# A two-layer graph network: its two node stages, run over chunks of seven blocks before, run block by block after, with their constants folded into the weights

## The chip, the cores and the metric

One core of a Trainium2 chip. The metric is the device time of one launch in microseconds (us).

## The reference, cut to what matters

There are 6250 nodes with 128 channels and 100,000 edges, each with 16 attributes. Linear layers are written as functions here.

```
msg  = relu(relu(m1(x)[src] + m2(x)[dst] + me(edge_attr)) @ W_net.T + b_net)   # 96 channels an edge
agg  = segment_max(msg, src)                   # 96 channels a node, 0 where none
x    = layernorm(x + x @ W_o1.T + b_o1 + agg @ W_o2.T + b_o2)      # first node stage
h    = gelu(concat(x[src], x[dst]) @ eW1 + eb1);  message = h @ eW2 + eb2
aggregated = segment_sum(message, dst)
upd  = gelu(concat(x, aggregated) @ nW1 + nb1) @ nW2 + nb2
x    = layernorm(x + (x + upd))                                     # last node stage
```

`layernorm` takes mean and variance over the 128 channels of a node, adds 1e-5 to the variance and divides by its root.

## The kernel before, in words

All numbers are float32 where nothing else is said. Nodes lie in NB = 49 blocks of 128; the edges pass in G = 208 groups of four steps of 128. The kernel is a row of stages, each a block of five engine programs (PE is TensorE, DVE VectorE, ACT ScalarE, POOL GpSimd, SP the DMA queue engine) that meet at its end: preparation; edges into the order of `src` (POOL scatters rows to DRAM, L938); the edge network with a running maximum per node (ending at 1780 us of the profile); **the first node stage** (L1252 to L1434); the second layer's edges, which gather rows of the table `a_d` that the first node stage wrote, and sum into `hsumT` and `deg` (1910 to 2973 us); **the last node stage** (L1551 to L1704). In a stage every engine runs its own program in order; semaphores alone tie the engines to one another. `wait(...)` and `wait_ge` stall the engine that meets them and all that stands behind them on it. Buffers in PSUM are pairs, used by turns (`ps_y[b % 2]` and so on).

**First node stage before.** POOL gathers, per block, 128 rows of the running maximum by index (`agg_all`, L1297; 49 gathers), and after them clears `hsumT` and `deg`. SP loads seven weight and bias tiles, then `x` and `xT` in seven parts each. The 49 blocks are cut into seven chunks of CH = 7. Within a chunk PE turns `agg` (`turn`, L1363), ACT copies it out (`aggregate`, L1328), PE multiplies `x` by `wo1` and `agg` by `wo2` (`update`, L1370, L1372), and DVE adds `x` with the biases (`add`, L1405; the biases go onto `x` at L1415). Once all seven blocks of the chunk are there, DVE takes the statistics of all (L1425, L1428), ACT the root of all (L1352), DVE the reciprocal (L1430) and the scaled rows `x1` (L1433). While the next chunk is summed, PE turns `x1` (`turn_x1`, L1377), ACT copies it (`turned`, L1339), PE makes the two tables of the second layer (`tables`, L1383), and ACT (`tables`, L1335) and DVE (`dst_table`, L1409) take them out of PSUM. SP stores `arow` a chunk at a time (L1317); the next stage begins when the last store has landed.

**Last node stage before.** SP loads seven weights (L1598). PE multiplies `ew2` and `eb2` by `nw1b` (L1668, L1669), ACT copies the products (L1694, L1695), DVE makes `x1 = 2 x1 + nb2` for all blocks (L1643). Then, by block: DVE a diagonal matrix of `deg` (`diagonal`, L1618), PE three products into `ps_k` (`hidden`, L1675 to L1680), ACT gelu (L1700), PE the product with `nw2` two blocks later (`update`, L1685), DVE the sum and the statistics (L1627, L1631, L1635). When all 49 blocks are there, one root on ACT (L1704, with a table load), one reciprocal (L1654), and then 49 scaled blocks on DVE (`normed`, L1659), stored seven at a time by SP (L1605, L1608).

## Time and profile before

| | us |
|---|---|
| median of three runs (least, most) | 3049.49 (3048.7, 3050.09) |
| the profiled execution, its own time | 3050.75 |
| its span, first to last instruction | 3048.9 |
| from the first gather of the first node stage to the next stage's first instruction | 1783.9 to 1909.8 |
| last node stage, first instruction to the end of the span | 2973.5 to 3048.9 |

Times inside a profile are microseconds from its first instruction. A timeline row reads: start, how long, engine, source line, operation, output tile <- input tiles, shape, how many such instructions in a row, and in brackets how long the engine had stood idle and what ended that.
### The profile page before, as it was taken

What the parts mean: (1) busy time and instruction counts of PE and PEld (TensorE: products, weight loads), DVE (VectorE), ACT (ScalarE), POOL (GpSimd) and SP (SyncE); (2) the same over time, 40 slices, a digit from 0 to 9 for tenths busy, and PEclk for the clock granted to TensorE, in tenths of its full rate; (3) what the DMA queues carried; (4) which work ended last, traced back from release to release, by engine and by line L of the source; (5) the groups of instructions that cost most, each with busy time, mean ns of one, the idle gap of its engine ahead of it and who ended that gap; (6) DMA issues with size and microseconds to landing.
All of it is one profiled execution on the core that took longest, in us unless ns stands there. A gap on an engine that the chain in (4) does not pass through costs nothing. (4 is left out here: it accounts for less than half of the span.)

```text
span 3048.9 us, 90135 instructions
## 1 busy us (share of the span) xinstructions
PE 2534.9 (83%) x22735; PEld 2063.0 (68%) x22736; DVE 2075.4 (68%) x9832; ACT 1020.7 (33%) x2227; POOL 1886.7 (62%) x2587
## 2 busy tenths in 40 slices
PE   5868988888888888499999967788888888888876
PEld 5647776666666666377777755677777777777766
DVE  6968999999999999377777755344444444444437
ACT  6314444444444444144444432222222222222212
POOL 1007777777777777644444452777777777777750
PEclk8879999999999999699999988899999999999998
DMA  5012222222222222188898861222222222222251
GB/s 195 5 40 48 47 48 48 47 47 47 47 47 47 47 47 47 54 216 227 226 227 226 226 186 40 55 53 52 53 52 52 52 52 52 52 52 52 52 38 47
DMA packets 583653, 247.82 MB, mean 81 GB/s; under 512 B 506238, under 2 KB 553496, under 8 KB 583336
## 3 DMA queue, kind: packets, MB, share of 16 engines
q1 hardware_dynamic: 418304, 101.65, 16.3%
q0 software_dynamic: 54816, 97.94, 12.5%
q10 hardware_dynamic: 110472, 47.49, 5.5%
q8 instruction: 29, 0.48, 0.1%
q14 instruction: 32, 0.26, 0.0%
HBM read 151.83 MB, written 101.41 MB: 83 GB/s over the span
## 5 line engine op out<-in xcount | busy, mean ns | idle before, releaser
L1465 POOL DMA_INDIRECT a_rows<-src_table,idx x832 | 785.8, 945 | 312.8 <-issue 229.5
L938 POOL DMA_INDIRECT edge_in_src_order<-u,place x832 | 802.6, 965 | 281.7 <-issue 205.7
L1547 ACT ACTIVATE h<-ps_h 128x512 f32<-128x512 f32 x208 | 124.2, 597 | 828.1 <-PE ps_h L1519 828.1
L1514 PE MATMUL ps_h<-a_rows,ident 128*128 128x512 f32 x416 | 236.7, 651 | 191.3 <-DMA a_rows<-src_table,idx 191.3
L1154 POOL COPY m_s<-m 128x144 f32 x832 | 232.7, 323 | 246.7 <-PE ps_pre L1201 246.0
L1482 DVE TENSOR_TENSOR hsumT<-hsumT,ps_s 128x128 f32 x832 | 239.8, 288 | 182.8 <-issue 85.4
L1528 PE MATMUL ps_s<-ohd_f,h 128*128 128x128 f32 x1664 | 359.8, 306 | 0.0
L1177 DVE TENSOR_TENSOR_SCAN top<-same,top,ps_net 96x512 f32<-96x512 bf16 x207 | 264.1, 1276 | 98.0 <-PE ps_net L1208 97.7
L1490 DVE COPY idx<-src_s 128x4 int32 (+1 forms) x208 | 35.4, 171 | 393.6 <-DMA a_rows<-src_table,idx 390.5
L1519 PEld LDWEIGHTS ps_h<-bpart,dstT_b 128*128 128x128 f32 x1664 | 220.4, 193 | 102.0 <-issue 101.8
L1090 ACT COPY u<-ps_u 128x384 f32<-128x384 f32 x208 | 99.5, 478 | 539.8 <-DMA edge_in_src_order<-u,place 519.7
L1073 PE MATMUL ps_u<-we_s,attrT 128*128 128x384 f32 x416 | 185.1, 527 | 113.6 <-ACT u L1090 113.6
L1077 PEld LDWEIGHTS ps_u<-m,dstT 128*128 128x128 f32 x1664 | 209.2, 194 | 70.0 <-issue 60.2
L1529 PEld LDWEIGHTS ps_n<-onesf,ohd_f 128*128 128x128 f32 x1664 | 253.1, 192 | 0.0
L1528 PEld LDWEIGHTS ps_s<-ohd_f,h 128*128 128x128 f32 x1664 | 252.9, 192 | 0.0
L1529 PE MATMUL ps_n<-onesf,ohd_f 128*128 128x1 f32 x1664 | 233.9, 210 | 0.0
L1519 PE MATMUL ps_h<-bpart,dstT_b 128*128 x1664 | 221.9, 277 | 0.0
L1208 PE MATMUL ps_net<-msg,wnet_s 97*96 97x512 f32 x416 | 219.2, 609 | 0.0
L1077 PE MATMUL ps_u<-m,dstT 128*128 x1664 | 218.2, 275 | 0.0
L1514 PEld LDWEIGHTS ps_h<-a_rows,ident 128*128 128x128 f32 x416 | 62.5, 189 | 209.1 <-DMA a_rows<-src_table,idx 157.2
L996 DVE CUSTOM_DVE_ANT_0 junk<-ps_cnt,ohlo_a 128x128 bf16<-128x128 f32 x832 | 191.4, 285 | 12.3 <-PE ps_cnt L1047 10.5
L1226 ACT ACTIVATE msg<-ps_pre 96x512 f32<-96x512 f32 x208 | 123.3, 593 | 173.4 <-PE ps_pre L1201 173.4
(266 smaller groups left out, 5675.4 us busy)
## 6 DMA issues: line engine op xcount, KB each, us to landing
u_in<-edge_in_src_order SPq DMA_DIRECT2D x208, 192.0 KB, 3.4
running_max<-row ACTq DMA_DIRECT2D x208, 192.0 KB, 4.1
rowt<-src_row SPq DMA_DIRECT2D x208, 130.0 KB, 3.7
key_in<-edge_keys SPq DMA_DIRECT2D x832, 2.0 KB
attr_in<-edge_attributes SPq DMA_DIRECT2D x832, 8.0 KB
edge_in_src_order<-u,place POOLq DMA_INDIRECT x832
a_rows<-src_table,idx POOLq DMA_INDIRECT x832
edge_attributes<-in_edge_attr ACTq DMA_DIRECT2D x8, 784.0 KB, 15.3
```

Source lines behind the costliest of these rows:

```text
L938: pool.indirect_dma_start(u_d, bass.IndirectOffsetOnAxis(place[:, u, j:j + 1], 0), ur[:, u, j, :], None).then_inc(sent[u], 16)
L996: v.tensor_tensor_reduce(junk2[:, j, :], ps_cnt[u % 2][:, j, :], ohlo[:, u, j, :], 1.0, 0.0, ALU.mult, ALU.add, across[:, u, j:j + 1]).the ...
L1077: mm = m.matmul(ps_u[:, j, :], dstT[:, u, j, :], m2[:, bass.ds(at[j], F)], start=False, stop=True, skip_group_check=True)
L1154: last = nc.gpsimd.tensor_copy(m1_s[:, u, j, :], m1[:].bitcast(F32)[:, bass.ds(at[j], 3 * F // 2)])
L1177: v.tensor_tensor_scan(top[:, u, :], same[:, u, :], ps_net[u % 2][:], 0.0 if first else top[:, (u - 1) % 4, 4 * P - 1:4 * P], ALU.mult, AL ...
L1208: m.matmul(ps_net[u % 2][:], wnet_s[:], msg[:, u, :], start=True, stop=True).then_inc(net_ready, 1)
L1465: pool.indirect_dma_start(a_rows[:, u, j, :], None, a_d, bass.IndirectOffsetOnAxis(idx[:, u, j:j + 1], 0)).then_inc(got[u], 16)
L1482: adds.add(v.tensor_tensor(at, at, ps_s[k][:, j, :], ALU.add))
L1514: m.matmul(ps_h[k][:].rearrange("p j d -> p (j d)"), ident[:], a_rows[:, u].rearrange("p j d -> p (j d)"), start=True, stop=False, skip_gr ...
L1519: mm = m.matmul(ps_h[k][:, j, :], dstT[:, k, j, :], bpart[:, bass.ds(at[j], D)], start=False, stop=True, skip_group_check=True)
L1528: m.matmul(ps_s[k][:, j, :], h[:, u, j, :], ohd[:, u, j, :], start=True, stop=True)
L1529: mm = m.matmul(ps_n[k][:, j:j + 1], ohd[:, u, j, :], onesf[:, 0:1], start=True, stop=True)
```

## The change

- The weights of the first node stage are loaded on ACT's queue at the start of the stage that scatters the edges, and POOL adds the identity to `wo1` there, so that one product gives `x + x W_o1`. `xT` is loaded once, in the preparation, and kept; `x` itself is not loaded any more. Two rows of ones under `aggT` and two rows under `wo2` bring in both biases.
- The first node stage is one loop over blocks. Every engine handles, in each turn t, parts of the blocks t to t - 4. The statistics read PSUM; root, reciprocal and shift are taken per block; ACT scales the block out of PSUM. POOL waits, before a gather, for the gather four blocks earlier. DVE clears `hsumT` and `deg` at the stage's start. SP loads the last stage's weights, and PE and ACT combine them at the stage's end.
- The last node stage begins with its loop. POOL makes the diagonals and adds half of `nb2` to `x1`; DVE's sum doubles it. The product with `nw2` comes one block later, not two. DVE computes the root by three Newton steps, for the blocks 0 to 6, 7 to 13, ... to 41, then 42 to 45, 46 and 47, and 48; ACT scales the blocks, one per turn; SP stores the same parts.

The diff, cut to its core: leading blanks and declarations are left out, and the lines it takes away stand in the functions printed above.

```diff
+pool.wait_ge(node_w_in, 16 * 6)
+nc.gpsimd.tensor_tensor(wo1_s[:], wo1_s[:], ident[:], ALU.add).then_inc(wo1_set, 1)
...
+for to, of in ((wo1_s[:], wo1), (wo2_s[0:F, :], wo2), (wo2_s[F:F + 2, :], bo),
+               (ew1_s[:, 0:D], ew1a), (ew1_s[:, D:2 * D], ew1b), (eb1_s[:], eb1.broadcast_to([P, D]))):
+    act.dma_start(to, of).then_inc(node_w_in, 16)
...
+stores = [b for b in range(CH, NB, CH) if b < NB - 3] + [b for b in (NB - 3, NB - 1, NB) if b > 0]
...
+    wait(pool, agg_in[b % 4], 16 * (b // 4))
     pool.indirect_dma_start(agg_all[:, b, :], None, s_d,
+                            bass.IndirectOffsetOnAxis(last_i[:, b:b + 1], 0)).then_inc(agg_in[b % 4], 16)
...
 s = nc.scalar
+def normed(b):
+    act.wait_ge(shift_ready, b + 1)
+    s.activation(x1[:, b, :], ps_y[b % 2][:, 0:D], ACT.Identity, bias=shift[:, b:b + 1],
+                 scale=rstd[:, b:b + 1]).then_inc(x1_ready, 1)
 def aggregate(b):
     act.wait_ge(agg_turned, b + 1)
     wait(act, y_ready, b - 1)
+    s.copy(aggT[0:F, b % 2, :], ps_t[b % 2][0:F, 0:P]).then_inc(aggT_ready, 1)
 def turned(b):
     act.wait_ge(x1_turned, b + 1)
     s.copy(x1T[:, P * b:P * b + P], ps_x[b % 2][:, 0:P]).then_inc(x1T_ready, 1)
+def tables(b):
+    act.wait_ge(ab_ready, b + 1)
+    s.copy(arow[:, b, :], ps_ab[b % 2][:, 0:D]).then_inc(a_ready, 1)
+def deviation(b):
+    act.wait_ge(var_ready, b + 1)
+    s.activation(std[:, b:b + 1], mv[:, b, 1:2], ACT.Sqrt, bias=eps_c[:]).then_inc(std_ready, 1)
+act.wait_ge(ones_set, 2)
+for t in range(NB + 3):
+    for lag, stage in ((2, normed), (0, aggregate), (2, turned), (3, tables), (1, deviation)):
+        if 0 <= t - lag < NB:
+            stage(t - lag)
+act.wait_ge(combined, 1)
+s.copy(w2n_s[:], ps_t[0][:, 0:D])
+s.copy(b2n_s[:], ps_t[1][:, 0:D])
...
 def turn(b):
+    pe.wait_ge(agg_in[b % 4], 16 * (b // 4 + 1))
     wait(pe, aggT_ready, b - 1)
     m.transpose(ps_t[b % 2][0:F, 0:P], agg_all[:, b, :], ident[:]).then_inc(agg_turned, 1)
 def update(b):
     to = ps_y[b % 2][:, 0:D]
+    wait(pe, x1_ready, b - 1)
     m.matmul(to, x1T[:, P * b:P * b + P], wo1_s[:], start=True, stop=False)
     pe.wait_ge(aggT_ready, b + 1)
     m.matmul(to, aggT[:, b % 2, :], wo2_s[:], start=False, stop=True).then_inc(y_ready, 1)
 def tables(b):
     pe.wait_ge(x1T_ready, b + 1)
+    wait(pe, a_ready, b - 1)
     wait(pe, b_ready, b - 1)
+    m.matmul(ps_ab[b % 2][:, 0:2 * D], x1T[:, P * b:P * b + P], ew1_s[:], start=True, stop=True).then_inc(ab_ready, 1)
+pe.wait_ge(wo1_set, 1)
+pe.wait_ge(ones_set, 2)
+for t in range(NB + 3):
+    for lag, stage in ((0, turn), (1, update), (2, turn_x1), (3, tables)):
+        if 0 <= t - lag < NB:
+            stage(t - lag)
+pe.wait_ge(last_w_in, 16 * 7)
+pe.wait_ge(aggT_ready, NB)
+m.matmul(ps_t[0][:, 0:D], ew2_s[:], nw1b_s[:], start=True, stop=True)
+m.matmul(ps_t[1][:, 0:D], eb2_s[:].broadcast_to([D, P]), nw1b_s[:], start=True, stop=True).then_inc(combined, 1)
...
 v = nc.vector
+v.memset(aggT[F:F + 2].rearrange("f k p -> f (k p)"), 1.0).then_inc(ones_set, 1)
+v.memset(eps_c[:], EPS_LN).then_inc(ones_set, 1)
+v.memset(hsumT[:], 0.0)
+v.memset(deg[:], 0.0)
 def dst_table(b):
     dve.wait_ge(a_ready, b + 1)
     v.tensor_tensor(bpart[:, D * b:D * b + D], ps_ab[b % 2][:, D:2 * D], eb1_s[:], ALU.add).then_inc(b_ready, 1)
+def variance(b):
+    dve.wait_ge(y_ready, b + 1)
+    v.bn_stats(stats[:, b, :], ps_y[b % 2][:, 0:D]).then_inc(stats_ready, 1)
+    dve.wait_ge(stats_ready, b + 1)
+    v.bn_aggr(mv[:, b, :], stats[:, b, :]).then_inc(var_ready, 1)
+def scaling(b):
+    dve.wait_ge(std_ready, b + 1)
+    v.reciprocal(rstd[:, b:b + 1], std[:, b:b + 1]).then_inc(r_ready, 1)
+    dve.wait_ge(r_ready, b + 1)
+    v.scalar_tensor_tensor(out=shift[:, b:b + 1], in0=mv[:, b, 0:1], scalar=-1.0, in1=rstd[:, b:b + 1],
+                           op0=ALU.mult, op1=ALU.mult).then_inc(shift_ready, 1)
+for t in range(NB + 4):
+    for lag, stage in ((2, scaling), (4, dst_table), (1, variance)):
+        if 0 <= t - lag < NB:
+            stage(t - lag)
...
+g = nc.gpsimd
+def diagonal(b):
+    wait(pool, k_ready, b - 3)
+    g.tensor_scalar(diag[:, b % 4, :], ident[:], deg[:, b:b + 1], None, ALU.mult).then_inc(diag_ready, 1)
+def half_bias(b):
+    g.tensor_tensor(x1[:, b, :], x1[:, b, :], nb2_s[:, 0, :], ALU.add).then_inc(biased, 1)
+g.tensor_scalar(nb2_s[:, 0, :], nb2_s[:, 0, :], 0.5, None, ALU.mult).then_inc(halved, 1)
+diagonal(0)
+diagonal(1)
+pool.wait_ge(halved, 1)
+for b in range(NB):
+    half_bias(b)
+    if b + 2 < NB:
+        diagonal(b + 2)
...
 def result(b):
+    dve.wait_ge(biased, b + 1)
     dve.wait_ge(o_ready, b + 1)
+    v.scalar_tensor_tensor(out=x1[:, b, :], in0=x1[:, b, :], scalar=2.0, in1=ps_o[b % 2][:, 0:D],
+                           op0=ALU.mult, op1=ALU.add).then_inc(y_ready, 1)
+def variance(b):
+    dve.wait_ge(stats_ready, b + 1)
+    v.bn_aggr(mv[:, b, :], stats[:, b, :]).then_inc(var_ready, 1)
 def statistics(b):
     dve.wait_ge(y_ready, b + 1)
     v.bn_stats(stats[:, b, :], x1[:, b, :]).then_inc(stats_ready, 1)
+ch = Chain(dve, root_chain)
+def scaling(lo, hi):
+    dve.wait_ge(var_ready, hi)
+    y, h, q = root[:, lo:hi], half[:, lo:hi], square[:, lo:hi]
+    ch(v.tensor_scalar(h, mv[:, lo:hi, 1], EPS_LN, None, ALU.add))
+    ch(v.tensor_single_scalar(bits[:, lo:hi], h.bitcast(I32), 1, op=ALU.logical_shift_right))
+    ch.add(v.tensor_scalar(h, h, -0.5, None, ALU.mult))
+    ch(v.tensor_scalar(y.bitcast(I32), bits[:, lo:hi], -1.0, float(0x5F3759DF), ALU.mult, ALU.add))
+    for _ in range(3):
+        ch(v.tensor_tensor(q, y, y, ALU.mult))
+        ch(v.tensor_tensor(q, q, h, ALU.mult))
+        ch(v.scalar_tensor_tensor(out=y, in0=q, scalar=1.5, in1=y, op0=ALU.add, op1=ALU.mult))
+    v.scalar_tensor_tensor(out=shift[:, lo:hi], in0=mv[:, lo:hi, 0], scalar=-1.0, in1=y,
+                           op0=ALU.mult, op1=ALU.mult).then_inc(shift_ready, 1)
+for t in range(NB + 1):
+    for lag, stage in ((0, result), (1, variance), (0, statistics)):
         if 0 <= t - lag < NB:
             stage(t - lag)
+    if t in stores:
+        scaling(([0] + stores)[stores.index(t)], t)
...
+def hidden(b):
     wait(pe, hid_ready, b - 1)
+    to = ps_k[b % 2][:, 0:P]
+    m.matmul(to, nw1a_s[:], x1T[:, P * b:P * b + P], start=True, stop=False)
+    m.matmul(to, w2n_s[:], hsumT[:, P * b:P * b + P], start=False, stop=False)
     pe.wait_ge(diag_ready, b + 1)
+    m.matmul(to, b2n_s[:], diag[:, b % 4, :], start=False, stop=True).then_inc(k_ready, 1)
+def update(b):
     pe.wait_ge(hid_ready, b + 1)
     wait(pe, y_ready, b - 1)
+    m.matmul(ps_o[b % 2][:, 0:D], hid[:, b % 4, :], nw2_s[:], start=True, stop=True).then_inc(o_ready, 1)
+for t in range(NB + 1):
+    for lag, stage in ((0, hidden), (1, update)):
+        if 0 <= t - lag < NB:
+            stage(t - lag)
...
+def gelu(b):
     act.wait_ge(k_ready, b + 1)
     wait(act, o_ready, b - 3)
+    s.activation(hid[:, b % 4, :], ps_k[b % 2][:, 0:P], ACT.Gelu, bias=nb1_c[:]).then_inc(hid_ready, 1)
+def normed(b):
+    act.wait_ge(shift_ready, 1 + sum(hi <= b for hi in stores))
+    s.activation(yout[:, b, :], x1[:, b, :], ACT.Identity, bias=shift[:, b:b + 1],
+                 scale=root[:, b:b + 1]).then_inc(out_ready, 1)
+done = 0
+for t in range(NB):
+    gelu(t)
+    if done < t - 4 and done < max([0] + [hi for hi in stores if hi <= t - 4]):
+        normed(done)
+        done += 1
+for b in range(done, NB):
+    normed(b)
```

## Rows read from the trace of the kernel before

**Rows 1.** Windows, first node stage: busy PE, PEld, DVE, ACT, POOL; PEclk, DMA share, GB/s.
```profile
1797.00:1910.00 113.00, 79.35 (x392) 62.83 (x392) 64.24 (x261) 33.83 (x155) 42.61 (x41) 0.80 0.31 87
```

**Rows 2.** Timeline: start and end of the first node stage.
```profile
1783.92 1.01 POOL L1297 DMA_INDIRECT agg_all<-running_max,last_i  x1 [0.69 <-issue]
...
1797.47 0.63 PE L1363 MATMUL ps_t<-ident,agg_all 128*96 128x128 f32 x2 [18.04 <-DMA agg_all<-running_max,last_i]
...
1906.11 0.27 ACT L1335 COPY arow<-ps_ab 128x128 f32<-128x128 f32 x1 [1.31 <-PE ps_ab L1383]
...
1909.82 0.31 DVE L1490 COPY idx<-src_s 128x4 int32<-128x4 int32 x3 [3.12 <-PEq L1291]
```

**Rows 3.** The tile agg_all, first three gathers: issue to landing.
```profile
DMA to landing us min/median/max: 2.6/3.0/4.5
```

**Rows 4.** Timeline: the steady loop and the end of a chunk, first node stage.
```profile
1884.51 0.70 PE L1383 MATMUL ps_ab<-ew_s,x1T 128*128 128x256 f32 x2
...
1885.25 0.27 ACT L1335 COPY arow<-ps_ab 128x128 f32<-128x128 f32 x1 [0.63 <-PE ps_ab L1383]
...
1885.41 0.27 ACT L1339 COPY x1T<-ps_x 128x128 f32<-128x128 f32 x1
...
1885.73 0.30 PEld L1383 LDWEIGHTS ps_ab<-ew_s,x1T 128*128 128x128 f32 x2
...
1890.64 1.44 DVE L1425 BATCH_NORM_STATS2 stats<-x 128x6 f32<-128x128 f32 x7
...
1892.73 0.30 ACT L1352 ACTIVATE std<-mv,eps_c 128x7 f32<-128x7 f32 x1 [2.33 <-DVE mv L1428]
1893.06 0.20 DVE L1430 RECIPROCAL rstd<-std 128x7 f32<-128x7 f32 x1 [0.37 <-ACT std L1352]
```

**Rows 5.** Windows at half clock: a dense stretch, and the last chunk's second half.
```profile
1866.70:1870.10 3.40, 3.40 (x15) 2.77 (x14) 2.46 (x7) 0.61 (x4) 0.00 (x0) 0.50 0.00 0
1894.00:1904.20 10.20, 8.65 (x19) 4.30 (x18) 2.64 (x10) 2.43 (x11) 0.00 (x0) 0.50 0.01 2
```

**Rows 6.** Groups by form, ACT and DVE: busy, mean ns of one | idle before.
```profile
L1090 ACT COPY u<-ps_u 128x384 f32<-128x384 f32 x208 | 99.5, 478 | 539.8 <-DMA edge_in_src_order<-u,place 519.7 <-PE ps_u L1077 19.6 <-issue 0.5
L1700 ACT ACTIVATE hid<-ps_k,nb_c 128x128 f32<-128x128 f32 x49 | 18.0, 367 | 28.7 <-PE ps_k L1680 28.7
L1704 ACT ACT_TABLE_LOAD x1 | 1.3, 1283 | 0.0
L1484 DVE TENSOR_TENSOR deg<-deg,ps_n 128x1 f32 x832 | 124.0, 149 | 0.0
```

**Rows 7.** Groups by form, POOL.
```profile
L1154 POOL COPY m_s<-m 128x144 f32 x832 | 232.7, 323 | 246.7 <-PE ps_pre L1201 246.0 <-POOL msg L1146 0.7
L391 POOL TENSOR_TENSOR we_s<-bias_r 1x384 f32<-1x384 f32 x1 | 1.0, 992 | 0.0
L387 POOL TENSOR_TENSOR bias_r<-bias_r 1x96 f32<-1x96 f32 x1 | 0.4, 375 | 0.0
```

**Rows 8.** Timeline: DVE beside a POOL clear, and the same seven instructions later.
```profile
1845.77 5.34 POOL L1299 MEMSET hsumT<- 128x6272 f32 x1
...
1848.40 4.21 DVE L1433 TENSOR_SCALAR x<-x,mv,rstd 128x128 f32<-128x128 f32 x7
...
1879.36 1.88 DVE L1433 TENSOR_SCALAR x<-x,mv,rstd 128x128 f32<-128x128 f32 x7
```

**Rows 9.** Timeline of the last node stage: its start, two blocks of its loop, its end.
```profile
2979.20 0.80 PE L1668 MATMUL ps_g<-nw1b_s,ew_s 128*128 128x128 f32 x2 [9.88 <-DMA nb_s<-in_nb]
...
3019.48 0.29 DVE L1627 TENSOR_TENSOR x<-x,ps_o 128x128 f32<-128x128 f32 x1
...
3020.37 0.29 DVE L1627 TENSOR_TENSOR x<-x,ps_o 128x128 f32<-128x128 f32 x1
...
3030.03 7.26 DVE L1659 TENSOR_SCALAR yout<-x,mv_b,rstd_b 128x128 f32<-128x128 f32 x28
...
3044.90 0.45 SPq L1608 DMA_DIRECT2D out<-yout  x1
```

More of the change, by code:

```diff
@@ L192, in gnn @@
         rank_p = sb(whole, "rank_p", [HB, 4, 2, P], F16)
+        x1T = sb(whole, "x1T", [D, NP])
+        wo1_s = sb(whole, "wo1_s", [D, D])
+        wo2_s = sb(whole, "wo2_s", [F + 2, D])
+        ew1_s = sb(whole, "ew1_s", [D, 2 * D])
+        eb1_s = sb(whole, "eb1_s", [P, D])
         pads_set = sem(whole, "pads_set")
+        node_w_in = sem(whole, "node_w_in")
+        wo1_set = sem(whole, "wo1_set")
         layer0 = ExitStack()
@@ L1267, in gnn @@
                 ps_ab = [ps(t, f"ps_ab{k}", [P, 512]) for k in range(2)]
-                chunks = [list(range(c, min(c + CH, NB))) for c in range(0, NB, CH)]
-                C = len(chunks)
-                agg_in = [sem(t, f"agg_in{c}") for c in range(C)]
-                w_in = sem(t, "w_in")
-                x_in = [sem(t, f"x_in{c}") for c in range(C)]
-                eps_set = sem(t, "eps_set")
+                agg_in = [sem(t, f"agg_in{k}") for k in range(4)]
+                last_w_in = sem(t, "last_w_in")
+                ones_set = sem(t, "ones_set_x")
                 agg_turned = sem(t, "agg_turned")
@@ L1289, in gnn @@
                 b_ready = sem(t, "b_ready")
-                a_out = [sem(t, f"a_out{k}") for k in range(2)]
+                combined = sem(t, "combined")
+                a_out = sem(t, "a_out")
                 with nc.Block() as block:
@@ L1339, in turned @@
                             s.copy(x1T[:, P * b:P * b + P], ps_x[b % 2][:, 0:P]).then_inc(x1T_ready, 1)
-                        act.wait_ge(eps_set, 1)
-                        for c in range(C + 1):
-                            for q in range(CH + 1):
-                                if c < C and q < len(chunks[c]):
-                                    aggregate(chunks[c][q])
-                                if c > 0 and 0 < q <= len(chunks[c - 1]):
-                                    tables(chunks[c - 1][q - 1])
-                                if c > 0 and q < len(chunks[c - 1]):
-                                    turned(chunks[c - 1][q])
-                            if c < C:
-                                lo, hi = chunks[c][0], chunks[c][-1] + 1
-                                act.wait_ge(var_ready, hi)
-                                s.activation(std[:, lo:hi], mv[:, lo:hi, 1], ACT.Sqrt, bias=eps_c[:]).then_inc(std_ready, 1)
+                        def tables(b):
[12 more added lines that the diff above has]
+                        s.copy(b2n_s[:], ps_t[1][:, 0:D])
                     @block.tensor
@@ L1380, in tables @@
                             pe.wait_ge(x1T_ready, b + 1)
+                            wait(pe, a_ready, b - 1)
                             wait(pe, b_ready, b - 1)
-                            to = ps_ab[b % 2]
-                            m.matmul(to[:, 0:2 * D], x1T[:, P * b:P * b + P], ew1_s[:], start=True, stop=True).then_inc(ab_ready, 1)
-                        for c in range(C + 1):
-                            for q in range(CH + 1):
-                                if c < C and q < len(chunks[c]):
-                                    turn(chunks[c][q])
-                                if c > 0 and q < len(chunks[c - 1]):
-                                    turn_x1(chunks[c - 1][q])
-                                if c < C and 0 < q <= len(chunks[c]):
-                                    update(chunks[c][q - 1])
-                                if c > 0 and 0 < q <= len(chunks[c - 1]):
-                                    tables(chunks[c - 1][q - 1])
+                            m.matmul(ps_ab[b % 2][:, 0:2 * D], x1T[:, P * b:P * b + P], ew1_s[:], start=True, stop=True).then_inc(ab_ready, 1)
[9 more added lines that the diff above has]
+                        m.matmul(ps_t[1][:, 0:D], eb2_s[:].broadcast_to([D, P]), nw1b_s[:], start=True, stop=True).then_inc(combined, 1)
                     @block.vector
@@ L1631, in statistics @@
                             v.bn_stats(stats[:, b, :], x1[:, b, :]).then_inc(stats_ready, 1)
-                        def variance(b):
-                            dve.wait_ge(stats_ready, b + 1)
-                            v.bn_aggr(mv[:, b, :], stats[:, b, :]).then_inc(mv_ready, 1)
-                        for b in range(4):
-                            if b < NB:
-                                diagonal(b)
-                        dve.wait_ge(w_in, 16 * 7)
-                        for lo in range(0, NB, CH):
-                            hi = min(lo + CH, NB)
-                            v.scalar_tensor_tensor(out=x1[:, lo:hi, :], in0=x1[:, lo:hi, :], scalar=2.0,
-                                                   in1=bcast(nb2_s[:], P, hi - lo, D), op0=ALU.mult, op1=ALU.add).then_inc(doubled, 1)
@@ L1645, in _ @@
-                        dve.wait_ge(doubled, -(-NB // CH))
-                        for t in range(NB + 6):
-                            for lag, stage in ((6, variance), (5, statistics), (4, result), (0, later_diagonal)):
+                        ch = Chain(dve, root_chain)
[12 more added lines that the diff above has]
+                                                   op0=ALU.mult, op1=ALU.mult).then_inc(shift_ready, 1)
@@ L1657, in normed @@
-                        def normed(b, u, n):
-                            one = bass.ds(b, 1)
-                            v.tensor_scalar(yout[:, one, :].rearrange("p a f -> p (a f)"), x1[:, one, :].rearrange("p a f -> p (a f)"),
-                                            mv[:, one, 0:1].rearrange("p a f -> p (a f)"), rstd[:, one], ALU.subtract, ALU.mult).then_inc(out_ready, 1)
-                        pipeline(dve, NB, [(0, normed)])
+                            if t in stores:
+                                scaling(([0] + stores)[stores.index(t)], t)
```

180 lines of the change are left out of this document (37 added, 143 removed).

## The prediction, on record before any result

> **What bounds the kernel now.** The windows over the first node stage come first [rows 1]: in 113 us PE is busy 79, DVE 64, ACT 34, POOL 43. No engine is full, so the order of the waits sets the pace, and the timeline has to be read. At its start [rows 2] the first gather goes out at 1783.9, PE's first product waits until 1797.5, since a chunk needs seven gathers; the last copy is at 1906.1 and the next stage starts at 1909.8. In a chunk [rows 4] the table product comes every 1.22 us (1884.51 to 1885.73); after seven blocks PE waits while DVE and ACT do statistics (1890.64), root (1892.73) and reciprocal (1893.06). What I use is (1909.8 - 1797.5) / 49 = 2.29 us per block, all told. In the last stage [rows 9] PE waits for weights until 2979.2, then a block takes 0.89 us (3019.48 to 3020.37); the scaled rows begin only at 3030.0, after all blocks, and the last store goes out at 3044.9, 4.0 us before the span's end.
>
> Everything else, some 2850 us, is the same program before and after. The profiled execution took 3050.75 us, its span 3048.9; the median of the runs is 1.3 us below the profiled execution, and I take the gain off the median.
>
> **First node stage: its start.** Without chunks, PE begins when the first gather has landed, 3.0 us after its issue (2.6 to 4.5) [rows 3], not after 13.6. Four gathers may be under way, and the issue of one takes POOL 1.01 [rows 2]: a landing of 3.0 is under 4 x 1.01, so the new wait on POOL costs nothing, and at the pace found below POOL, which needs half of it, is ahead anyway. Behind that wait stand only more gathers. The loads of x and xT, which stood beside the gathers, are gone.
>
> **Its pace.** All engines run in order, so I look for the circle that must be passed once per block. It goes through ACT: it scales block b, PE turns it and then makes the tables of b-1, ACT copies the turned block and then the tables, and only then takes the root of block b+1, which DVE needs for reciprocal and shift, which ACT needs to scale b+1. The terms: ACT scales, with bias and scale, 0.37 (the gelu of the same size with a bias [rows 6]; a plain copy is 0.27 [rows 4]); PE turns (0.11) and streams the tables, 0.74 from the weight load to ACT's copy (1884.51 to 1885.25) [rows 4], together 0.85; the copy holds ACT for 0.16 (1885.25 to 1885.41); root 0.30 for seven columns, taken for one; reciprocal 0.16, between 0.15 [rows 6] and 0.20 [rows 4]; shift 0.15 [rows 6]; four hand-overs of 0.03 to 0.04 (1892.73 + 0.30 to 1893.06) [rows 4], 0.14. The sum is 2.13; 2.1 is taken, since the turn's stream hides the first weight load; 1.9 to 2.3 are the ends. So the pipeline by block runs at 2.1 us, far from the 1.22 of PE.
>
> **Its sum.** Gather 3.0; block 0 through turn, product, statistics, root to the scaled row 2.4; 48 x 2.1 = 100.8; the last block's turn and tables 2.1; the table load 1.3 [rows 6]; PE begins at half clock after its idle time, 1.0; DVE clears hsumT, on POOL 5.3 us [rows 8], and holds back either the first statistics or the first gather, 1.4 (0 to 4): 112.0. From 1783.9 that is 1895.9; the end as before, 3.4 from the last copy, gives 1899.3. Against 1909.8: **10.5 gained**. The products of the last stage's weights, 1.3 us, lie beside the last store. With the ends of the pace and the clearing: 1 to 21.
>
> **Moved into the scattering stage.** Six weight loads are issued on ACT's queue ahead of its loop, about 0.45 us each (the last stage's single issue at the end is as long [rows 9]), 2.7 us; ACT idles 539.8 us there behind landings and products [rows 6], and at that stage's start it has no input yet. Uncovered they would cost 2.7 once, and POOL's addition of the identity 0.44. I take nothing.
>
> **Last node stage: its start.** No loads and no products: PE starts when POOL has made the first diagonal, 0.7 us after the stage's beginning at 2973.5, in place of 5.7.
>
> **Its loop.** PE: 49 x 0.89 = 43.8 and 2.7 for the first blocks at half clock (PE has been idle). POOL: addition of 128 columns by the slope of two POOL additions [rows 7], (992 - 375) / 288 = 2.14 ns a column, 0.375 + 32 x 0.00214 = 0.44; diagonal 0.30 (a copy of 144 is 0.32): 0.75 a block, under 0.89. With the ends 0.38 and 0.99 it would be 0.7 to 1.3, and then POOL is the bound; the slope decides for me. DVE: result, then statistics that wait for it, 0.53 a block, and per part 14 chained instructions of 0.155 + 0.035 [rows 4, 6], 2.66 us. Seven blocks cost DVE 3.7 + 2.7 = 6.4, PE 6.2. PE can go on for two blocks during a chain, about 1.5 us, and stands for the rest: 1.15 x 6 = 6.9.
>
> **The shared way into SBUF.** At 1848.40 DVE's seven scalings took 4.21 us; the same seven take 1.88 [rows 8]. POOL's clear ran until 1851.11, and DVE was through 1.5 us after it: DVE had stood for POOL. In the new loop POOL works 0.75 of every 0.89 us beside DVE. While a chain holds PE back, POOL has some three pairs of operations left to do, 2.2 us, which fall between the links; I take 1.6 a chain, 9.6 in all; the bounds are 0 and 12. The Trainium skill (SBUF — State Buffer, "SBUF: two separate sides") states the rule behind it: DVE in a two-port mode or with two SBUF inputs and GpSimd exclude each other for a whole instruction. By it nearly every link is held, the full 12; it speaks against this change, and the trace agrees in kind. What the rows leave open is whether operations of seven columns are held as those of 128.
>
> **Its end.** Three parts end close together: after the last result 0.5 for statistics, two chains 5.3, one scaled block 0.4, hand-overs: 6.5; a store of one part, 0.45 and about 2.1 (before: 4.0 in all with larger ones ahead of it). ACT's scaled rows lie beside the loop (gelu 0.37 and 0.37 under 0.89). Sum: 0.7 + 43.8 + 2.7 + 6.9 + 9.6 + 6.5 + 2.6 = 72.8, against 3048.9 - 2973.5 = 75.4: **2.6 gained**; 0 to 13 with the port's bounds, down to -4 if POOL's pair is dearer.
>
> **The sum.** 10.5 + 2.6 = 13.1; 3049.5 - 13.1 = **3036**.
>
> **Rivals.**
> - *The forecast's circle without the wait for the shared way*: the last stage gains 9.6 more, 12.2, and the total is 3027. For it: DVE's small operations beside POOL's gathers average 0.149 [rows 6]. Inside my range; 0.25.
> - *The pipeline reaches PE's or POOL's pace*, 1.25 a block (1.22 [rows 4] is the table product's pace now): 48 x 0.85 = 41 more, 2995. Against it stands the order in ACT's program. 0.04.
> - *POOL becomes the bound of the last stage*: a pair at 1.05 in place of 0.89 gives 49 x 0.16 = 8 more: 3044. 0.10.
> - *Half clock, the slower side.* Its place is the first node stage. There TensorE may stay at 1.2 GHz: at that level turn and tables stream 0.54 longer, the circle is 2.65, 48 x 0.54 = 26 more: **3062**. It decides from about 24 of the 48 blocks on. A stretch at 0.50 in which PE was busy throughout, 3.40 of 3.40, was followed by full clock; the last chunk, busy 8.65 of 10.20 with gaps, stayed at 0.50 [rows 5]. A block's products, 79.35 / 49 = 1.62 at a mean clock of 0.80 [rows 1], are 1.3 at full clock and 2.6 at half: nearly all of 2.65, as in the dense stretch, and so I think it is raised. 0.06.
> - *A table load at each change between root and scaling on ACT*: 98 x 1.28 = 125, 3161. Copies and gelu alternate without a load (one load in each such stage [rows 6]); Identity isn't in the trace. 0.01. The Trainium skill (ScalarE: Activation LUTs, "Table sets: the hidden batching unit") has identity in every set, which would exclude it; no row here shows it.
> - *The change does less than it says*: block by block, the circle is 2.3 and the Newton chains cost their full bounds, so that both take what the early starts give: 3049. 0.08.
>
> **How the numbers follow.** The forecast's own case, 3030 to 3042, has 0.46: it takes in 1.95 to 2.2 a block and 0 to 3 for each port wait. No port wait 0.25, PE's pace 0.04, POOL's bound 0.10, half clock 0.06, table loads 0.01, less than said 0.08: together 1. The range leaves out pace, clock and tables, 0.11, and some of the last case and of the tails: 3022 to 3048. A measurement here tells 0.2%, 6.1 us, from no change, so 3043.4 and 3055.6 are the borders. Faster: 0.46 + 0.25 + 0.04 and half of POOL's case, 0.80. Same: the other half, 0.08 for less than said and 0.01 for a clock that falls only for some blocks, 0.14. Slower: 0.05 and 0.01, 0.06.
>
> **What would show it.** Right: first product of the first node stage near 1787; a steady 2.1 us a block there with ACT's table copy waiting for PE; clock 1.00; the stage's end near 1899. In the last stage the first `hidden` near the stage's start, PE waiting for DVE once per part, DVE's chain links longer while POOL works. Wrong: a pace under 1.9 or over 2.3, PEclk 0.5 in the middle, gathers waiting on POOL, links of 0.19 throughout.

## The result, and the profile after

| | before | after |
|---|---|---|
| median of the runs of the comparison (six of each), us | 3050.26 | 3059.44 |
| ratio, 95% interval | | 1.0031 (1.0018 to 1.0044) |
| span of the profiled execution | 3048.9 | 3056.3 |
| first node stage, first gather to the next stage's first instruction | 1783.92 to 1909.82: 125.9 | 1780.80 to 1905.27: 124.5 |
| last node stage, first product or diagonal to the span's end | 2973.5 to 3048.9: 75.4 | 2970.2 to 3056.3: 86.1 |

The change makes the kernel 9 us slower, where 13 us less were forecast. The first node stage gives back nearly all that its early start brings, and the last one is 10.7 us longer. The stages ahead of the first node stage end 3.1 us earlier, and the stage between the two is 1.3 us longer: -3.12 - 1.43 + 1.29 + 10.68 = 7.42, the difference of the spans. A second pair of profiles (changed_third and before_third, below) has -0.3, -0.2, +5.3 and +10.9 there: the loss of the last stage comes again, the small differences ahead of it don't.

The timeline of the changed kernel, first node stage: its start, one block of the steady loop, its end (they answer to [rows 2] and [rows 4]).

```profile
1780.80 1.01 POOL L1307 DMA_INDIRECT agg_all<-running_max,last_i  x1 [15.98 <-POOLq L1144]
...
1781.80 5.29 DVE L1399 MEMSET hsumT<- 128x6272 f32 x1 [1.25 <-issue]
...
1783.39 0.42 PE L1364 MATMUL ps_t<-ident,agg_all 128*96 128x128 f32 x1 [6.83 <-DMA agg_all<-running_max,last_i]
...
1788.28 0.46 ACT L1329 ACTIVATE x<-ps_y,shift_x,rstd 128x128 f32<-128x128 f32 x1 [0.43 <-DVE shift_x L1416]
...
1893.26 0.46 ACT L1329 ACTIVATE x<-ps_y,shift_x,rstd 128x128 f32<-128x128 f32 x1 [0.42 <-DVE shift_x L1416]
...
1893.77 0.33 PE L1376 MATMUL ps_x<-ident,x 128*128 128x128 f32 x1 [0.88 <-ACT x L1329]
...
1893.93 0.61 PE L1382 MATMUL ps_ab<-ew_s,x1T 128*128 128x256 f32 x2
...
1894.57 0.27 ACT L1343 COPY arow<-ps_ab 128x128 f32<-128x128 f32 x1 [0.18 <-PE ps_ab L1382]
...
1894.73 0.30 ACT L1347 ACTIVATE std<-mv,eps_c 128x1 f32<-128x1 f32 x1
...
1895.06 0.16 DVE L1414 RECIPROCAL rstd<-std 128x1 f32<-128x1 f32 x1 [1.22 <-ACT std L1347]
1895.26 0.16 DVE L1416 SCALAR_TENSOR_TENSOR shift_x<-mv,rstd 128x1 f32<-128x1 f32 x1
...
1895.45 0.46 ACT L1329 ACTIVATE x<-ps_y,shift_x,rstd 128x128 f32<-128x128 f32 x1 [0.42 <-DVE shift_x L1416]
...
1902.59 0.27 ACT L1343 COPY arow<-ps_ab 128x128 f32<-128x128 f32 x1 [0.59 <-PE ps_ab L1382]
...
1905.27 0.31 DVE L1477 COPY idx<-src_s 128x4 int32<-128x4 int32 x3 [2.09 <-PEq L1302]
```

The circle, the loop of waits that the prediction describes, is there step by step: scaled, turned (0.51 later), tables, ACT's copy (0.80), root (0.16), reciprocal (0.33), shift (0.20), scaled again (0.19): 2.19 us. Of the 48 steps from one scaled block to the next, 34 take 2.20; 12 take 2.56 to 2.76 and one 2.25, since there PE runs at 1.2 GHz (the stretch from 1808.7 below has a clock of 0.71); the first takes 1.91.

Windows of the changed kernel (busy PE, PEld, DVE, ACT, POOL; PEclk, DMA share, GB/s): the first node stage, two pieces of it, then the last stage: a stretch without a chain, one behind a chain's stop, and the stage up to PE's end.

```profile
1784.00:1905.00 121.00, 78.58 (x395) 59.82 (x395) 48.77 (x247) 67.06 (x248) 43.71 (x47) 0.86 0.20 48
1801.80:1808.60 6.80, 4.02 (x25) 3.06 (x24) 2.90 (x16) 3.99 (x15) 4.99 (x6) 1.00 0.41 102
1808.70:1815.50 6.80, 4.89 (x20) 3.67 (x21) 2.62 (x14) 3.53 (x13) 5.28 (x6) 0.71 0.22 44
...
2976.00:2981.00 5.00, 5.00 (x47) 5.00 (x46) 3.42 (x18) 2.06 (x6) 5.00 (x11) 1.00 0.00 0
...
3010.20:3013.50 3.30, 3.30 (x20) 3.30 (x19) 1.26 (x7) 1.20 (x4) 1.41 (x3) 0.58 0.02 5
2970.20:3044.90 74.70, 58.54 (x392) 56.98 (x392) 50.07 (x230) 33.18 (x88) 49.96 (x99) 0.80 0.11 32
```

In the last stage PE is busy 58.5 of 74.7 us at a mean clock of 0.80; the kernel before did its products there in 46.9 (window 2979.2 to 3028.3 of its trace), a block per 0.89 us [rows 9]. PE's work has not grown, its clock has fallen. The timeline shows where: a chain on DVE, and PE behind it. A chain is the fourteen instructions that take the root of a part, nearly each waiting for the one before; one of them is called a link, and the time that PE stands still behind a chain a stop.

```profile
3015.68 0.45 POOL L1574 TENSOR_TENSOR x<-x,nb_s 128x128 f32<-128x128 f32 x1
...
3015.71 0.45 DVE L1623 TENSOR_SCALAR half<-mv_b 128x7 f32<-128x7 f32 x1
...
3017.69 0.46 POOL L1574 TENSOR_TENSOR x<-x,nb_s 128x128 f32<-128x128 f32 x1
3017.74 0.43 DVE L1628 TENSOR_TENSOR square<-root 128x7 f32<-128x7 f32 x1
...
3019.20 0.17 DVE L1629 TENSOR_TENSOR square<-square,half 128x7 f32<-128x7 f32 x1
...
3019.60 0.17 DVE L1631 SCALAR_TENSOR_TENSOR shift_y<-mv_b,root 128x7 f32<-128x7 f32 x1
...
3020.11 0.77 PE L1655 MATMUL ps_o<-nw_s,hid 128*128 128x128 f32 x2 [2.58 <-DVE x L1605]
...
3022.38 0.64 PE L1647 MATMUL ps_k<-x1T,nw1a_s 128*128 128x128 f32 x2
```

This chain takes 4.05 us (3015.71 to 3019.76). A link of seven columns that begins just after POOL's addition ends just with it (3018.17 beside 3018.15); a link alone takes 0.17. PE stops for 2.58 us, and then its pairs of 128 columns take 0.64 in place of 0.39. The starts of DVE's results show the whole pattern of a part: 4.45 to 5.69 us at each of the first five chains, one or two steps of about 0.53 to catch up, then up to three of 1.43 to 1.71 (half clock), then 0.89 again.

The groups by form of POOL and DVE in the last stage give the sizes that [rows 7] had to bound (busy, mean ns of one | idle before).

```profile
L1571 POOL TENSOR_SCALAR diag<-ident,deg 128x128 f32<-128x128 f32 x49 | 29.4, 600 | 19.8 <-PE ps_k L1650 19.8
L1574 POOL TENSOR_TENSOR x<-x,nb_s 128x128 f32<-128x128 f32 x49 | 22.1, 453 | 0.0
...
L1628 DVE TENSOR_TENSOR square<-root 128x7 f32<-128x7 f32 x18 | 6.7, 371 | 0.6
```

Its end, in the timeline: PE's last product, the last block's scaled row, the last store.

```profile
3044.49 0.49 PE L1655 MATMUL ps_o<-nw_s,hid 128*128 128x128 f32 x2 [0.23 <-ACT hid L1668]
...
3047.07 0.27 DVE L1605 SCALAR_TENSOR_TENSOR x<-x,ps_o 128x128 f32<-128x128 f32 x1
...
3052.87 0.49 ACT L1672 ACTIVATE yout<-x,shift_y,root 128x128 f32<-128x128 f32 x1 [1.78 <-DVE shift_y L1631]
3053.39 0.33 SPq L1594 DMA_DIRECT2D out<-yout  x1
```

### The profile page after: what moved, and what is told of

It is laid out like the page before. It is cut to its first block and busy times, and to the rows that moved or that the text cites. A ratio compares the mean times of both kernels' runs of the same rounds, so it can differ in the third digit from the quotient of the medians.

```text
span 3056.3 us, 90088 instructions
## 1 busy us (share of the span) xinstructions
PE 2546.3 (83%) x22735; PEld 2071.6 (68%) x22736; DVE 2060.6 (67%) x9841; ACT 1071.0 (35%) x2365; POOL 1931.5 (63%) x2683
## 5 line engine op out<-in xcount | busy, mean ns | idle before, releaser
L1004 DVE CUSTOM_DVE_ANT_0 junk<-ps_cnt,ohlo_a 128x128 bf16<-128x128 f32 x832 | 191.6, 285 | 11.3 <-PE ps_cnt L1055 9.2
```

What stands on the lines that cost most here:

```text
L1004: v.tensor_tensor_reduce(junk2[:, j, :], ps_cnt[u % 2][:, j, :], ohlo[:, u, j, :], 1.0, 0.0, ALU.mult, ALU.add, across[:, u, j:j + 1]).the ...
```

## The experiments

Theories: **the clock** (the chains stop PE, and the blocks behind each stop run at 1.2 GHz); **POOL's hold** (POOL's addition keeps DVE out, so the chain is long in the first place); for the first node stage, **the circle** through ACT's order. The sets came out at two levels. At the lower one the kernel before takes 3048 to 3053 us, at the upper one 3835 to 3873: there the stages of the scatters and gathers and the first node stage are longer, with waits that the trace lays on nothing in the kernel ("remote", "issue"). The expectations take the levels for two chips, but the chip's number on record doesn't part them: number 9 gave 3053 in one set and 3871 in the next. What does is open. The steady loops of both node stages have the same steps at both levels, so the lengths of loops can be read at either, the ratios only within a set.

**Only the first node stage changed.** The last stage's block is that of before, behind the changed first one.

> The first node stage of the changed kernel, with the last node stage of before (its own weight loads and products included). If the loss sits in the last stage alone, whose length went from 75.4 to 86.1 us, the time is 3059.4 - 10.7 = 3048.7, within 3 of before (3050.3). If moving the weights or the new first node stage costs something elsewhere, it stays above 3054.

It came at the upper level: 3839.03 against 3835.29, ratio 1.0013 (1.0002 to 1.0025). Its last stage is 77.9 us long, the changed one in the same set 82.7 (in root_earlier, next). So 4.8 us go with the last stage here, and the 3.7 us that stay are a little over the 3 of the first case. The whole change gives 1.0052 in another set (below); no unedited changed kernel ran in this one, so that this run doesn't show how much of the loss the last stage holds. At the lower level the two pairs of profiles do: 10.7 and 10.9 us.

**The root taken earlier.** In the first node stage:

```diff
-((2, normed), (0, aggregate), (2, turned), (3, tables), (1, deviation))
+((2, normed), (0, aggregate), (1, deviation), (2, turned), (3, tables))
```

> Only the order of ACT's five parts in a turn of the first node stage changes: the root is taken before the copies of the turned block and of the tables. Theory of the circle (normed, turn, tables, copy, root, reciprocal, shift; 2.20 us): it is broken, and the next one goes through DVE's statistics (0.5), root and two copies on ACT (0.7) and the table addition (0.3), 1.5 to 1.6 us a block. 48 x 0.6 = 29 less, and 6 more if the clock then stays at 1.00: 3024 (3015 to 3035). Rival: the pace is set by PE's own waits on the copies, which stand in the same order as before: within 5 us of 3059.

Ratio 0.9937 (0.9913 to 0.9961), and asked again:

> The changed kernel with the earlier root alone, as in the first set. First node stage 95 in place of 125.1, last stage 83 to 86: 3059.4 - 30 = 3029 (3026 to 3033) on a chip that gives 3050 for before. If the earlier root only moves the wait into the next stage's first gathers: 3040 or more.

This set too was at the upper level: 0.9947 (0.9931 to 0.9963). The first node stage takes 142.3 us in root_earlier, where first_new_last_old, in the same set, has 171.5. The steady steps are 1.49 and 1.66 by turns, 1.575 on the mean, in place of 2.20, and the clock stays at full speed (window of the steady loop):

```profile
2360.00:2424.00 64.00, 53.88 (x326) 41.54 (x326) 43.28 (x204) 50.05 (x202) 0.00 (x0) 1.00 0.16 44
```

The circle is broken as expected, the next one is where it was expected to be in length, and the clock's 6 us come along. The two expected times are for the lower level, where this edit didn't run alone.

**The chains spread.** The links of a part are issued one behind each of DVE's three steps of the following turns; ACT's scaled rows come two turns later; the last part has seven blocks.

```diff
+stores = list(range(CH, NB, CH)) + [NB]
...
 for t in range(NB + 1):
     for lag, stage in ((0, result), (1, variance), (0, statistics)):
         if 0 <= t - lag < NB:
             stage(t - lag)
+        if t < NB:
+            link()
     if t in stores:
         scaling(([0] + stores)[stores.index(t)], t)
+        while t >= NB and links:
+            link()
```

Here `scaling` only appends its fourteen instructions to `links`, and `link` waits for the last one and issues the next.

> The root of seven blocks in the last stage is spread over the turns that follow, up to three links a turn, so that DVE never holds PE back for a chain; the last seven blocks form one part. Clock theory (the chains stop PE, and after each stop PE runs some blocks at 1.2 GHz): no stop, clock 1.00, and the stage runs at POOL's pair, 1.0 us a block: 4 + 48 + 10 of tail = 62 in place of 86, 3035 (3030 to 3040). Rival, DVE's small operations are held by POOL wherever they stand: DVE needs 1.1 to 1.3 a block, 3042 to 3050, with PE still waiting for DVE.

Ratio 0.9967 (0.9954 to 0.9980). The last stage takes 65.7 us, the same stage unedited 82.7 there. PE's clock is 0.99 over the loop (3762 to 3812). While POOL works, a turn of three links takes 0.98 to 1.6 and one without links 0.89, but for one in each part of 1.30, where ACT took up scaled rows a turn too early and kept PE waiting, 0.63 in the later parts. In the turns of 1.00 DVE has no gap, with links of 0.35 beside POOL's additions, and POOL has none either (its pair, 0.60 + 0.45, comes every 1.00). So the stops and the clock went as the clock theory says, and what sets the 1.00, POOL's pair or POOL's hold on the links, stays open between the theory and its rival. Both need POOL's additions: without them (all_fixed_again, below) the steady turns take 0.89, links or not.

**PE kept busy.** Ten products into an unused bank in each of the first six waits; DVE and POOL are as they were.

```diff
+                            if b - 2 in stores[:-3]:
+                                for _ in range(10):
+                                    m.matmul(ps_z[:, 0:P], nw1a_s[:], x1T[:, 0:P], start=True, stop=True)
                             wait(pe, y_ready, b - 1)
```

> Ten more products of 128 columns into an unused bank are put where PE waits in each of the first six chains of the last stage; nothing else changes. Clock theory: PE never idles long, PEclk stays at 1.00 from the first chain on, the blocks of 1.71 us go to 0.89: 8 to 12 us less, 3047 to 3051. Rival, the stops themselves and POOL's hold on the links are the whole loss: 3059 or slower, since the added products (10 x 0.215 = 2.2 us) fill a wait of 2.5 and no more.

Ratio 0.9992 (0.9980 to 1.0005), the stage 75.4 us, where root_earlier, with the unedited last stage, has 82.7 in the same set and the first profile 86.1. The window over its loop:

```profile
3760.00:3823.00 63.00, 58.85 (x499) 57.55 (x498) 50.85 (x244) 34.40 (x93) 46.51 (x93) 0.98 0.14 39
```

The steps at a chain are nearly as long as before (4.11 to 4.99), but behind them come 0.51, 0.85, 0.89 and none of 1.71. The stage is 7 to 11 us shorter; the six steps at the chains hold 2.0 of the 7 and 1.1 of the 11 (26.3 us together, beside 28.3 and 27.4), the rest, 5 to 10 us, is the clock's share.

**The half bias moved into the first node stage.** POOL adds it once a block has been turned; in the last stage only the diagonals are left to it.

```diff
+                        for b in range(NB):
+                            pool.wait_ge(x1_turned, b + 1)
+                            g.tensor_tensor(x1[:, b, :], x1[:, b, :], nb2_s[:, 0, :], ALU.add)
...
                         for b in range(NB):
-                            half_bias(b)
-                            if b + 2 < NB:
-                                diagonal(b + 2)
+                            diagonal(b)
```

> Half of nb2 is added by POOL in the first node stage, once a block has been turned, so that in the last stage POOL works 0.60 of a block in place of 1.05. If POOL's instructions hold DVE's links, a chain of seven goes from 4.0 to 4.1 us (6 of them) to 3.2 to 3.4, and the first one, 5.24, to the same: 5 to 7 us less than the unedited changed kernel. If the chain's length is its own, it stays at 4.0 and the time within 2. In both cases the clock still falls after each chain.

> The changed kernel with nothing edited, beside the others of this set: on a chip that gives 3050 for the kernel before, 3057 to 3062; with the last stage 86 us long, of which some 25 at 1.2 GHz.

bias_early 0.9988 (0.9978 to 0.9998), changed_again 1.0052 (1.0036 to 1.0069), same set, at the upper level. The last stage falls from 82.7 to 66.4. All six chains of seven take 2.72 to 2.77 us, in the timeline of bias_early with a diagonal beside them:

```profile
3814.78 0.60 POOL L1577 TENSOR_SCALAR diag<-ident,deg 128x128 f32<-128x128 f32 x1 [0.26 <-PE ps_k L1646]
3814.81 0.17 DVE L1626 SCALAR_TENSOR_TENSOR root<-square,root 128x7 f32<-128x7 f32 x1
...
3815.01 0.17 DVE L1624 TENSOR_TENSOR square<-root 128x7 f32<-128x7 f32 x1
...
3816.80 0.46 PE L1651 MATMUL ps_o<-nw_s,hid 128*128 128x128 f32 x2 [1.23 <-DVE x L1601]
```

The expectation for bias_early undershot, in the chain (3.2 to 3.4) and in the gain (5 to 7 us), and its last sentence is wrong: PE's stop is 1.23, and the clock does not fall at all behind it (the window 3806 to 3861 has 0.99, and no step of 1.71). The stage gives 16 us; the medians of the two kernels lie 22 apart, and the rest isn't traced. So the 16 us are both theories in one row: POOL's additions make the chain 1.3 us longer, that makes PE's stop twice as long, and the longer stop costs, behind most of them, the clock.

**Both repairs, and all together.** both_fixed has the earlier root and the spread chains (ACT's rows one more turn later); all_fixed also the moved half bias and the last three rows on DVE; statistics_earlier adds DVE's order (2, scaling), (1, variance), (4, dst_table).

> The earlier root of the first node stage and the spread chains of the last one together, with ACT's scaled rows one turn later. Both causes are independent if the stages only add up: first node stage 48 x (2.32 - 1.575) = 36 less, last stage 86.1 - 65.7 = 20 less and 1 for ACT's turn: 57 less than the changed kernel, 3002, and 48 less than before. Rival: the gathers (1.25 us each) or the next stage's start take a part back: 3010 to 3020.

> As both_fixed, with the half bias in the first node stage and the last three blocks scaled by DVE beside ACT. If POOL's pair of 1.05 us sets the spread loop's pace of 1.00, the pace falls to PE's 0.89: 48 x 0.11 = 5 less, and 1 for the tail: 2996. If DVE's links set it, or the additions disturb the first node stage: 3002 or more.

At the upper level 0.9903 (0.9886 to 0.9919) and 0.9901 (0.9884 to 0.9919), 37 to 41 us less than before. The next set was at the lower level:

> The kernel before, unedited, with a profile of the same chip as its neighbours: it shows what of the longer times there lies in stages that no kernel of this study touches. If that chip gives 3835 again, the scatter and gather stages are to hold 700 of the 785 us more, and the first node stage, which gathers too, more than 126.7; if it gives 3050, all rows are to be as in the first profile within 3 us.

> The combined version once more, timed in more rounds. From the steady rows: first node stage 1.575 a block in place of 2.33, last stage 56.7 in place of 75.4 to 86.1. On a chip that gives 3050 for before: 2992 to 2998. On one that gives 3840 or more: 35 to 45 less than before, as in the last set.

> On top of the combined version, DVE takes a block's statistics before it makes the table of three blocks earlier. If the circle of 1.575 us goes through that table addition (it waits for ACT's last copy and holds the statistics back by 0.3), the pace falls to what PE needs, 1.25 to 1.35: 48 x 0.27 = 13 less than the combined version. If ACT's own work (five parts a turn) sets it: within 3.

before_again 1.0004 (0.9994 to 1.0015), all_fixed_again 3019.44 (2992 to 2998 were expected), 0.9885 (0.9867 to 0.9904), statistics_earlier 3017.38, 0.9891 (0.9875 to 0.9908). The node stages did what the rows said: from POOL's first gather 94.5 us, last stage 57.2, every block at 0.89, and statistics_earlier's steady pace is the same 1.49 and 1.66, so DVE's table addition is not in the circle; what sets this pace no run shows. (Its first node stage is 90.8 us; all_fixed_again has one step of 4.53 in it, told of at the end.) But 34 us are gained where the two stages are 50 shorter. The groups by line on POOL (busy, mean ns of one | idle before) say where the rest went; all_fixed_again, then before_again:

```profile
L944 POOL DMA_INDIRECT edge_in_src_order<-u,place x832 | 811.3, 975 | 276.0 <-issue 198.4 <-DVE place L1027 53.8 <-ACT u L1098 23.5
L1460 POOL DMA_INDIRECT a_rows<-src_table,idx x832 | 799.3, 961 | 258.8 <-issue 244.0 <-PE ps_h L1514 8.2 <-DVE idx L1485 6.6
```

```profile
L938 POOL DMA_INDIRECT edge_in_src_order<-u,place x832 | 802.2, 964 | 282.1 <-issue 202.8 <-DVE place L1019 77.0 <-ACT u L1090 1.9
L1465 POOL DMA_INDIRECT a_rows<-src_table,idx x832 | 785.9, 945 | 312.9 <-issue 236.2 <-DVE idx L1490 59.9 <-PE ps_h L1519 16.8
```

A scatter takes 975 ns in place of 964 and a gather 961 in place of 945; 832 of each make 22 us. For the scatters the same is seen at the upper level: 991 and 989 in bias_early and all_fixed, where the kernels without the moved half bias have 972 to 979. The gathers don't tell there: 969 and 971 in these two, 948 to 969 in the others.

**Without the moved half bias.**

> The earlier root and the spread chains, with the half bias where the change has it, on a chip that is hoped to give 3050 for before. Rows so far: first node stage 95 in place of 126, last stage 63.2 in place of 75.4. If the longer gathers of the combined version (975 and 961 ns in place of 965 and 945, 832 of each) come from moving the half bias, they are 965 and 945 here, and the time is 3050 - 31 - 12 = 3007 (3002 to 3011). If they come from any edit of the first node stage, 3025 to 3030.

> As both_fixed_again, with the last three blocks scaled by DVE beside ACT. ACT's seven rows of the last part take 2.8 us after the last chain; four take 1.65: 1.1 less than both_fixed_again in the last stage, which the times can hardly tell (3006).

> As both_fixed_again, with 49 one-column clears of an unused tile on POOL in the first node stage, each behind the wait that the half bias had there. If a longer POOL program alone makes every gather and scatter 11 to 16 ns longer, the same is seen here, also in the stages before: 22 us more than both_fixed_again. If the addition itself or its place in memory does it: within 3.

The upper level again: 0.9903 (0.9887 to 0.9918), 0.9899 (0.9883 to 0.9915) and 0.9913 (0.9899 to 0.9927). The three rows on DVE shorten the last stage from 65.6 to 62.9, in the times nothing. A longer POOL program with the same waits leaves the scatters at 975 and the gathers at 957 where both_fixed_again has 974 and 969: the length of the program is not what makes the scatters slower. The expectation of both_fixed_again could not be settled at this level. Then, at the lower one:

> The same kernel as both_fixed_again, asked again for a chip that gives 3050 for before, since its neighbours of the earlier sets ran on one that gives 3835 to 3873: there 3002 to 3011, with gathers of 965 and 945 ns. If the gathers are as long as in the combined version there, 3025 to 3030.

> The changed kernel unedited, on the same chip as the kernel above and the one below: 3057 to 3062 where before gives 3050 (its gathers 965 and 945 ns), 15 to 20 more than before on the other chip, as in the second set.

> The kernel before with a profile. Where it gives 3835 or more, this shows whether its first node stage stands as long beside the gathers as that of the changed kernel does there (176.8 us in place of 125.1): 170 to 185 if the stops come with the gathers whatever the kernel, 130 if they belong to the change.

both_fixed_third **3001.57 us, ratio 0.9847 (0.9833 to 0.9860)**; changed_third 3059.68, 1.0034 (1.0022 to 1.0046); before_third 1.0005 (0.9995 to 1.0016). This version, at the near end of what was expected (3002 to 3011), beats both kernels, by 46 and 58 us (48 and 57 were the sums for both_fixed). Its first node stage takes 88.9 us from its first instruction to the next stage (125.5 in before_third), its last one 65.3 (75.7), its scatters and gathers 964 and 946 ns. Windows over its two loops:

```profile
1789.00:1866.00 77.00, 63.89 (x377) 49.34 (x376) 50.94 (x241) 61.61 (x239) 40.76 (x44) 0.97 0.26 69
2941.00:2992.00 51.00, 47.16 (x381) 44.71 (x380) 45.79 (x229) 30.95 (x84) 46.68 (x93) 0.97 0.13 37
```

What before_third was to settle, whether the kernel before stands as long in its first node stage at the upper level, stays open, since it came at the lower.

## Why the prediction was wrong

**The step that failed** is "Its loop. PE: 49 x 0.89 = 43.8 and 2.7 for the first blocks at half clock". The forecast had PE idle for 17.2 us up to its last product (0.7 + 6.9 + 9.6), and PE is idle 16.2 of 74.7. But it priced the products as if the clock stayed up: 46.5 us, and they took 58.5. Those 12 us are more than the 10.7 by which the stage grew. The rival *half clock* was looked for in the first node stage alone, where PE runs thin; in the last stage the stops were in the sum and their consequence was not. pe_filled shows it alone: nearly the same stops, filled with products, and no step of 1.71 behind them; the stage is 5 to 10 us shorter by that, so that not all of the 12 comes back.

**POOL's hold** was named, taken at 1.6 us a chain, and measured at 4.05 - 2.77 = 1.3; the step at a chain fell from 4.45 to 3.22 without the additions. Right in kind and size; and the stop that is left without them, 1.23, is what the sum had (1.15). Of POOL's pair the addition was right (0.45 for 0.44); the diagonal takes 0.60, where a copy's 0.32 [rows 7] stood for it, so that the pair is 1.05, over PE's 0.89. The condition of the rival *POOL becomes the bound* was thus met from the start. The stops hid it, and the steps of 1.00 in chain_spread fit it as well as they fit held links.

**The first node stage**, 115.4 forecast, 124.5 measured. The circle was right, step by step: 2.13 summed, 2.1 taken, 2.20 measured; the scaling from PSUM takes 0.46, not 0.37. 48 x 0.1 = 4.8. A further 6 us (111.6 between first and last scaled row, less 48 x 2.2) are blocks at half clock, which the sum left out: the rival priced a stage wholly at half clock, and a clock that falls only for some blocks had a chance of 0.01. The start was 1.6 shorter (7.5 for 9.1), the end 5.4 for 5.5. The table loads of the rival did not come: the stage has one, of 1.28 us, though ACT goes from root to scaling to copies in every block.

**The tail**, 9.1 forecast, 11.3 measured: the chain of blocks 42 to 45 stands ahead of the results of 47 and 48, so that the last result comes 2.1 us after PE's last product, and then two chains follow.

Together 9.1 + 12.0 - 1.0 + 2.2 = 22.3 us in the two stages; 23.4 lie between forecast and median. By this sum half clock is 18 of them, 12 in the last stage and 6 in the first. What was moved ahead of the first node stage cost nothing that the rows show, as forecast: the stages ahead end 3.1 and 0.3 us earlier in the two pairs of profiles. The stage between the two node stages is 1.3 and 5.3 us longer; the forecast had nothing there, and the cause stays open.

Of what would show it, first product (2.6 us after the first gather), circle, wait for DVE once per part and long links were all seen; the clock of 1.00 and the end near 1899 were not, and the warning sign of a clock at half in the middle of the stage was there. The range, 3022 to 3048, took the clock in the first stage as one case of 0.06 and had no term for it in the last.

## What to carry to other kernels

A stop of PE costs itself and can cost the clock of what follows: where a chain must hold PE back, read what the granted clock does behind the stops, of which the length alone doesn't tell, and spread the chain over turns or fill the stop. In a loop over in-order engines, write down the circle through each engine's order before cutting it into single blocks: here one tuple moved forward was worth 29 us in the first node stage. And a helper engine's spare time is not free while DVE runs chains of tiny operations beside it.

## What the runs showed of the hardware

- **A one-column operation of DVE can wait for a burst of POOL's.** In all_fixed_again POOL catches up on its additions after the gathers; ordinary shifts take 0.16, beside the burst 0.32 to 0.49, and one took 3.20 us and ended with the burst (the row of POOL has the 19 of its 43 additions that the view holds):

```profile
1861.68 7.88 POOL L1316 TENSOR_TENSOR x<-x,nb_s 128x128 f32<-128x128 f32 x19
...
1866.37 3.20 DVE L1424 SCALAR_TENSOR_TENSOR shift_x<-mv,rstd 128x1 f32<-128x1 f32 x1
```

The prediction had left open whether operations of a few columns are held. They are, and here over several of POOL's instructions, not one. It is one case: beside a like burst in statistics_earlier no shift took over 0.45. The Trainium skill (SBUF — State Buffer, "SBUF: two separate sides") lets whoever comes first hold the pair for its instruction; by that rule the wait would have ended with one addition, 0.46. Beside POOL's diagonals, which also read SBUF, links took 0.17 to 0.31; the rule alone doesn't tell additions from diagonals, and no run here explains it.
- **The length of a stop alone doesn't tell what the clock does behind it.** The six stops of bias_early, 1.17 to 1.23 us, left it at 2.4 GHz. Five profiles have the changed last stage as it is (the first one, changed_again, changed_third, root_earlier and its repeat). Of their 20 stops of 2.42 to 2.75 us, 18 were followed by 1.2 GHz and two, of 2.64 us, were not, though the third of 2.64 was. Sixth stops of 1.85 and 1.87 us left the clock up, those of 1.96, 2.06 and 2.17 did not. In changed_again, the 3 us behind a stop of 2.44 and behind one of 2.64, and the first products behind the second:

```profile
3833.54:3836.54 3.00, 3.00 (x14) 3.00 (x15) 1.74 (x10) 0.93 (x3) 0.85 (x2) 0.50 0.03 8
3844.11:3847.11 3.00, 3.00 (x27) 3.00 (x28) 2.45 (x13) 1.73 (x6) 1.76 (x4) 1.00 0.00 0
...
3844.11 0.46 PE L1655 MATMUL ps_o<-nw_s,hid 128*128 128x128 f32 x2 [2.64 <-DVE x L1605]
3844.41 0.39 PE L1647 MATMUL ps_k<-x1T,nw1a_s 128*128 128x128 f32 x2
```

- **The moved half bias lengthens the mean scatter and gather of the whole program**, also in the stages ahead of it, by 11 and 16 ns at the lower level and the scatters by 10 to 19 at the upper. The length of POOL's program doesn't do it. The cause stays open.
- **The same program took 3048 to 3053 us in three sets and 3835 to 3873, a quarter more, in three others**, with scatters and gathers that cost POOL nearly the same (945 to 979 ns) but wait longer between them, and with waits of 8 to 18 us in the unrolled first node stage while the gathers run. One chip's number stands in both groups; the cause wasn't tried.
